# Gathered expert tiles turned by 32x32 block transposes on VectorE instead of on TensorE

## The reference

```python
h = einsum('bsi,boi->bso', x, cond_weight[adapter_ids])          # 1024 x 1024 per batch
shared = silu(h @ Wg_s.T) * (h @ Wu_s.T) @ Wd_s.T                # inner width 1024
probs = softmax(h @ gate_w.T); top 2 of 16, weights normalised
for each expert e:  silu(h @ Wg_e.T) * (h @ Wu_e.T) @ Wd_e.T     # inner width 256
out = x + shared + sum over the token's two experts, weighted
```

## Time and profile before

| | us |
|---|---|
| median of 3 runs (lowest, highest) | 1130.09 (1129.95, 1130.22) |
| span of the profiled execution | 1131.0 |
| TensorE busy | 1108.0 |
| VectorE busy | 567.2 |
| ScalarE busy | 475.7 |
| POOL busy | 166.3 |
| mean traffic of the DMA engines | 219 GB/s |

### The profile page before, as it was taken

The page is one execution under the profiler, slowest core; times in us unless marked ns, Lnnn a source line. Parts: engine busy times, 40 slices in busy tenths (PEclk is TensorE's granted clock), DMA queues, the critical chain, the costliest instruction groups (busy, mean ns, idle before and its releaser), DMA issues.

```text
span 1131.0 us, 16957 instructions
## 1 busy us (share of the span) xinstructions
PE 1108.0 (98%) x5250; PEld 917.4 (81%) x5251; DVE 567.2 (50%) x638; ACT 475.7 (42%) x602; POOL 166.3 (15%) x250
## 2 busy tenths in 40 slices
PE   8999999999999999999999999999999999999996
PEld 7788888888887888888888887788888888888885
DVE  6556555436764445654644544444462355344452
ACT  6556564433233455665645555532331223132210
POOL 1112121000011111111111111041003110032041
PEclk9999999999999999999999999999999999999998
DMA  9787786521256568787786887364256534464264
GB/s 352 291 317 273 266 307 228 198 75 75 89 210 224 191 227 312 252 309 255 293 307 221 310 309 274 124 247 154 92 225 234 213 111 197 156 223 162 79 223 148
DMA packets 40931, 247.45 MB, mean 219 GB/s; under 512 B 4994, under 2 KB 5122, under 8 KB 30594
## 3 DMA queue, kind: packets, MB, share of 16 engines
q1 hardware_dynamic: 14530, 154.15, 36.0%
q0 software_dynamic: 20032, 71.31, 18.4%
q10 hardware_dynamic: 6336, 21.56, 5.1%
HBM read 201.39 MB, written 49.81 MB: 222 GB/s over the span
## 4 chain that ended last, share of the span: by engine, by line
PE 95%; issue 1%; ACT 1%; DVE 1%; DMA 1%; ACTq 0%; DVEq 0%; SPq 0%
PE bank L516 30%; PE bank L518 30%; PE bank L517 29%; PE bank L684 3%; PE bank L537 1%; PE bank L529 1%; PE bank L717 1%; DMA raw<-cond_w 1%; ACT w_split_sb L798 0%; DVE w_split_sb L1050 0%; ACTq L248 0%; ACT y_out L798 0%; ACT hT_hi L798 0%; DVE tile_hT L1050 0%; DVE e_act L1336 0%
## 5 line engine op out<-in xcount | busy, mean ns | idle before, releaser
L1050 DVE TENSOR_TENSOR w_split_sb<-raw,w_split_sb 128x2048 fp32r<-128x2048 f32 (+3 forms) x152 | 259.2, 1728 | 92.9 <-ACT w_split_sb L798 92.0
L798 ACT ACTIVATE w_split_sb<-raw 128x2048 fp32r<-128x2048 f32 (+3 forms) x152 | 218.2, 1463 | 95.3 <-PE bank L518 85.3
L516 PE MATMUL bank<-hT_hi,w_split_sb 128*128 128x512 f32 x512 | 200.0, 391 | 0.9 <-ACT y_out L798 0.9
L517 PE MATMUL bank<-hT_lo,w_split_sb 128*128 128x512 f32 x512 | 199.4, 389 | 0.0
L518 PE MATMUL bank<-hT_hi,w_split_sb 128*128 128x512 f32 x512 | 199.4, 389 | 0.0
L516 PE MATMUL bank<-w_split_sb,tile_hT 128*128 (+1 forms) x312 | 125.7, 403 | 3.8 <-issue 2.6
L518 PE MATMUL bank<-w_split_sb,tile_hT 128*128 (+1 forms) x312 | 122.5, 393 | 0.0
L517 PE MATMUL bank<-w_split_sb,tile_hT 128*128 (+1 forms) x312 | 122.5, 393 | 0.0
L516 PEld LDWEIGHTS bank<-hT_hi,w_split_sb 128*128 128x128 f32 x512 | 96.1, 188 | 21.2 <-issue 1.3
L517 PEld LDWEIGHTS bank<-hT_lo,w_split_sb 128*128 128x128 f32 x512 | 96.1, 188 | 19.9
L518 PEld LDWEIGHTS bank<-hT_hi,w_split_sb 128*128 128x128 f32 x512 | 96.1, 188 | 19.9
(11 more groups left out here) (149 smaller groups left out, 1529.1 us busy)
## 6 DMA issues: line engine op xcount, KB each, us to landing
raw<-sh_gu_w SPq DMA_DIRECT2D x16, 2048.0 KB, 9.0
raw<-exp_gu_w SPq DMA_DIRECT2D x16, 2048.0 KB, 8.7
raw<-cond_w SPq DMA_DIRECT2D x14, 2048.0 KB, 8.6
y_dram<-y_out ACTq DMA_DIRECT2D x39, 512.0 KB, 6.1
raw<-sh_down_w SPq DMA_DIRECT2D x8, 2048.0 KB, 7.9
raw<-exp_down_w SPq DMA_DIRECT2D x16, 1024.0 KB, 7.3
h_dram<-h_row POOLq DMA_DIRECT2D x32, 256.0 KB, 6.0
x_raw_sb<-xT SPq DMA_DIRECT2D x7, 1024.0 KB, 11.0
```

What stands on the lines that cost most here:

```text
L516: nc.tensor.matmul(dst, lhs[0], rhs[0], start=first, stop=False)
L517: nc.tensor.matmul(dst, lhs[0], rhs[1], start=False, stop=False)
L798: return nc.scalar.activation(dst, src, ACT.Copy)
L1050: return nc.vector.tensor_tensor(dst, src, hi.bitcast(F32), ALU.subtract)
```

## The change

The eight transposes per tile leave TensorE. The rows of a tile are gathered in four indirect DMAs: the one with number i brings, to the 32 partitions of group j, quarter j (256 values) of the rows of slots 32 i to 32 i + 31. One VectorE instruction then turns each 32x32 block of the 128x1024 tile, from `h_in[par]` to a new float32 buffer `tile_f32[par]` in the upper half of `raw[1]`. This yields the values of a token along the partitions in another order than before (group j holds quarter j), and the gate-up weights are brought in the same order, by four DMAs of 32 partitions each, every one in runs of 4 KB. ScalarE and VectorE split the turned tile from SBUF in one instruction each, ahead of the silu and the product, and no longer from PSUM. `gather_h` waits for the turn of the tile that last used the buffer. Row numbers (4 x token + quarter) come from four small matmuls with a spreading matrix and one VectorE instruction behind the meta steps (`route_rows`). The last gather, of a tile never used, is left out. The second shared weight load waits for the last tile's split, as the turned tiles share its buffer.

```diff
+            def expert_gu_load(e):
+                by_block = exp_gu_w[bass.ds(e, 1), :, :].rearrange("o (b k) (j n) -> j (o k) b n", k=32, j=BLOCKS)
+                for j in range(BLOCKS):
+                    sp.dma_start(raw[0][32 * j:32 * (j + 1), :].rearrange("k (b n) -> k b n", b=BLOCKS), by_block[j]).then_inc(e_raw_gu, 16)
+
             sp.wait_ge(w_split, POST + 1)
-            sp.dma_start(raw[0][:, :], exp_gu_w[0]).then_inc(e_raw_gu, 16)
+            expert_gu_load(0)
...
             sp.wait_ge(ed_split, EXPERTS)
+            sp.wait_ge(et_lo, 2 * run + 3)
             sp.dma_start(raw[1][:, :], sh_gu_w[1]).then_inc(raw_in[1], 16)
...
-            wait(routed, 1)
+            wait(rows_known, 1)
             wait(a_lo, FB + 2)
             for m in range(2):
                 wait(h_store[m], 16 * QUARTERS * UPQ // 2)
 
+            h_blocks = h_dram.rearrange("t (j c) -> (t j) c", j=BLOCKS)
+
             def gather_h(s, par):
-                wait(et_mm, 2 * s + 2)
-                nc.gpsimd.tensor_copy(idx_h[par][:, :], small["tok_idx"][:, bass.ds(s, 1)]).then_inc(idx_ready, 1)
+                wait(e_turned, s + 1)
+                nc.gpsimd.tensor_copy(idx_h[par][:, :], small["row_idx"][:, bass.ds(s, 1), :].rearrange("p o i -> p (o i)")).then_inc(idx_ready, 1)
                 wait(idx_ready, s + 1)
-                nc.gpsimd.indirect_dma_start(
-                    out=h_in[par][:, :], out_offset=None, in_=h_dram,
-                    in_offset=bass.IndirectOffsetOnAxis(ap=idx_h[par][:, 0:1], axis=0)).then_inc(h_gather[par], 16)
+                for i in range(BLOCKS):
+                    nc.gpsimd.indirect_dma_start(
+                        out=h_in[par][:, i, :], out_offset=None, in_=h_blocks,
+                        in_offset=bass.IndirectOffsetOnAxis(ap=idx_h[par][:, i:i + 1], axis=0)).then_inc(h_gather[par], 16)
 
             gather_h(0, 0)
             gather_h(1, 1)
...
-            def transpose_tile(s, par, count, first_bank=4):
-                pe.wait_ge(h_gather[par], 16 * count)
-                for hf in range(2):
-                    pe.wait_ge(et_lo, 2 * s + hf + 1)
-                    for i in range(4):
-                        k = 4 * hf + i
-                        last = nc.tensor.transpose(bank[first_bank + hf][:, i * P:(i + 1) * P], h_in[par][:, k * P:(k + 1) * P], ident[:, :])
-                    last.then_inc(et_mm, 1)
-
-            def gate_up_tile(s, par, e1, odd, hT_of=None, between=None):
-                pe.wait_ge(et_lo, 2 * s + 4)
+            def spread_tokens(m):
+
+                if m == 1:
+                    pe.wait_ge(rt_tokf, 1)
+                    for i in range(BLOCKS):
+                        last = nc.tensor.matmul(bank[7][:, 128 + i * TPAD:128 + (i + 1) * TPAD], rt["spread"][:, i, :],
+                                                rt["tok_f"][:, :], start=True, stop=True)
+                    last.then_inc(rt_spread, 1)
+
+            def gate_up_tile(s, par, e1, odd, hT_of=None):
+                pe.wait_ge(et_lo, s + 1)
...
-            def tile_step(s, par, nxt_count):
+            def tile_step(s, par):
 
                 (_, e1_before, odd_before), (_, e1, odd) = load_meta(mybir.EngineType.PE, s - 1, 2)
                 gate_up_tile(s, par, e1, odd)
-                transpose_tile(s + 1, 1 - par, nxt_count)
                 down_tile(s - 1, 1 - par, e1_before, odd_before)
                 transpose_act(s, par)
 
-            def first_transposes(m):
-
-                if m == 1:
-                    pe.wait_ge(routed, 1)
-                    transpose_tile(0, 0, 1, first_bank=6)
-
-            shared_down(0, COND_CHUNKS + 4, 0)
-            shared_down(0, COND_CHUNKS + 5, 1, first_transposes)
-
-            def second_transposes():
-                pe.wait_ge(d_ev, 2 * QM + 2)
-                transpose_tile(1, 1, 1)
+            shared_down(0, COND_CHUNKS + 4, 0, spread_tokens)
+            shared_down(0, COND_CHUNKS + 5, 1)
 
             pe.wait_ge(s_mul, FB + 2)
-            pe.wait_ge(routed, 2)
+            pe.wait_ge(routed, 1)
             run = pairs_to_run(pe)
-            gate_up_tile(0, 0, 1, 0, tile0_hT, second_transposes)
+            gate_up_tile(0, 0, 1, 0, tile0_hT)
             transpose_act(0, 0)
             with pe.Fori(0, PAIRS) as i:
                 with pe.If(run > i):
-                    tile_step(2 * i + 1, 1, i + 2)
-                    tile_step(2 * i + 2, 0, i + 2)
-            tile_step(2 * run + 1, 1, run + 2)
-            tile_step(2 * run + 2, 0, run + 2)
+                    tile_step(2 * i + 1, 1)
+                    tile_step(2 * i + 2, 0)
+            tile_step(2 * run + 1, 1)
+            tile_step(2 * run + 2, 0)
 
 
             pe.wait_ge(hT_split, 4)
...
-            def tile_hi(s, dst, first_bank=4):
-                for hf in range(2):
-                    act.wait_ge(et_mm, 2 * s + hf + 5)
-                    copy(dst[:, 0, 4 * hf:4 * hf + 4, :].rearrange("p k t -> p (k t)"), bank[first_bank + hf][:, :]).then_inc(et_hi, 1)
+            def tile_hi(s, par, dst):
+                act.wait_ge(e_turned, s + 3)
+                copy(dst[:, 0, :, :], tile_f32[par][:, :, :]).then_inc(et_hi, 1)
...
+                if not last:
+                    act.wait_ge(gu_mm, s + 2)
+                    tile_hi(s + 1, 1 - par, tile_hT[1 - par])
                 if split_hT:
                     hT_hi_parts(16, (0, 1))
                 silu_tile(s, par)
-                tile_hi(s + 1, tile_hT[1 - par])
                 if split_hT:
...
             def route_tokens():
+                step(nc.vector.tensor_copy(rt["spread"][:, :, :].rearrange("p i (j t) -> p i j t", t=32),
+                                           ident[:, :].rearrange("p (i t) -> p i t", t=32).unsqueeze(2).to_broadcast([P, BLOCKS, BLOCKS, 32])))
                 dve.wait_ge(rt_tok, 1)
-                nc.vector.tensor_copy(small["tok_idx"][:, :], bank[7][:, 64:64 + TPAD]).then_inc(routed, 1)
+                nc.vector.tensor_copy(rt["tok_f"][:, :], bank[7][:, 64:64 + TPAD]).then_inc(rt_tokf, 1)
+
+            def route_rows():
+                dve.wait_ge(rt_spread, 1)
+                nc.vector.tensor_scalar(small["row_idx"][:, :, :].rearrange("p t i -> p i t"),
+                                        bank[7][:, 128:128 + BLOCKS * TPAD].rearrange("p (i t) -> p i t", i=BLOCKS),
+                                        float(BLOCKS), small["block_of"][:, 0:1], ALU.mult, ALU.add).then_inc(rows_known, 1)
 
             def route_start():
                 logits_out(QUARTERS - 1)
...
-            def tile_lo(s, dst, first_bank=4):
-                for hf in range(2):
-                    dve.wait_ge(et_hi, 2 * s + hf + 1)
-                    lo(dst[:, 1, 4 * hf:4 * hf + 4, :].rearrange("p k t -> p (k t)"), bank[first_bank + hf][:, :],
-                       dst[:, 0, 4 * hf:4 * hf + 4, :].rearrange("p k t -> p (k t)")).then_inc(et_lo, 1)
-
-            tile_lo(0, tile0_hT, first_bank=6)
+            def tile_turn(par, count):
+                dve.wait_ge(h_gather[par], 16 * BLOCKS * count)
+                nc.vector.transpose(tile_f32[par][:, :, :].rearrange("p (b a) (i t) -> p i a b t", a=2, t=32),
+                                    h_in[par][:, :, :].rearrange("p i (a b c) -> p i a b c", a=2, c=32)).then_inc(e_turned, 1)
+
+            def tile_lo(s, par, dst):
+                dve.wait_ge(et_hi, s + 1)
+                lo(dst[:, 1, :, :], tile_f32[par][:, :, :], dst[:, 0, :, :]).then_inc(et_lo, 1)
+
+            tile_turn(0, 1)
+            tile_lo(0, 0, tile0_hT)
...
-            def tile_step(s, par, last=False, split_hT=False):
+            def tile_step(s, par, count, last=False, split_hT=False):
                 (new_before, e1_before, odd_before), (new, e1, odd) = load_meta(mybir.EngineType.DVE, s - 1, 2)
                 act_lo(s - 1, 1 - par)
+                if not last:
+                    tile_turn(1 - par, count)
                 with dve.If(new_before == 1):
                     expert_d_lo(2 * WD - odd_before * (2 * WD), 2 * e1_before)
                 if last:
...
                 else:
                     with dve.If(new == 1):
                         expert_gu_lo(2 * CH - odd * (2 * CH), 4 * e1, (0, 1))
+                if not last:
+                    tile_lo(s + 1, 1 - par, tile_hT[1 - par])
                 if split_hT:
                     hT_lo_part(0, 0)
                     hT_lo_part(0, 1)
                 mul_tile(s, par)
-                tile_lo(s + 1, tile_hT[1 - par])
                 if split_hT:
                     hT_lo_part(0, 2)
```

More of the change, by code:

```diff
@@ L94, in adaln_ffn_kernel @@
     tile0_hT = at("tile0_hT", [P, 2, KT, P], F32R, 176)
+    tile_f32 = [at(f"tile_f32{i}", [P, KT, P], F32, 24 + 4 * i) for i in range(2)]
     rows_q3 = [at(f"rows_q3{m}", [P, HID], F32, 144 + 4 * m) for m in range(QM)]
@@ L105, in adaln_ffn_kernel @@
     hT_raw = [at(f"hT_raw{i}", [P, 4, P], F32, 192 + 2 * i) for i in range(4)]
```

(8 more changed lines are left out.)

49 lines of the change are left out of this document (26 added, 23 removed).

## The result

The changed kernel takes 1159.98 us in the median (1152.29 to 1161.69), the kernel before 1130.22 beside it: a ratio of 1.0249, with a 95% interval from 1.0231 to 1.0266. It is slower, and by more than the range allowed. Its profiled execution is the quickest of five, 1152.29 us with a span of 1150.8, so the trace explains 20 of the 30 us; the other four had spans of 1157.9 to 1160.2 us, and no trace of them is there.

The account below looks back on a forecast made before the run. TensorE was taken as the bound (busy 98% of the span, 95% of the chain). Slower gate-up loads, +25.7 us, and removed transposes, -17.4, summed to +8.3 on the median 1130.09: 1138 us, range 1102 to 1150 for 8 in 10.

Parts of the forecast that it names:

- the likeliest case: Gate-up load slowed by about half, making the kernel slower: 1138 us, own range 1126 to 1150, chance 0.55.
- The gate-up load: Four DMAs to 32 partitions take 11 us for 5.5, landing 14.2 us after issue: +25.7 us over eight intervals.
- The eight: Intervals between gate-up load issues behind two-tile experts, 151.1 us together before, forecast at 22.1 us each, 176.8 in all.
- the run length costs nothing: Gate-up load in 4 KB runs for 16 KB: no cost, as y stores in 4 KB runs moved 0.374 MB per us.
- 20 x 0.87 = -17.4 us: Loop steps outside the eight slow cycles and the last two each gain the removed transposes' 0.87 us on TensorE.
- Cost nothing, with 0.2 us of cover: Turn on VectorE in splitting steps: product ready at 8.1 us, TensorE asks for it at 8.3, so no wait.
- ScalarE: "nothing": ScalarE's copy of the turned tile, ahead of the silu, ends at 5.7 us of a step and costs nothing.
- The turn at 1.2 us: VectorE's 128x1024 turn per tile takes 1.2 us, by the nearest row, with bounds of 0.65 and 2.4 us.
- The gathers: "nothing, with 1.9 us of cover": Four gathers per tile on POOL: buffer full after 13.8 us, wanted 15.7 us on, so no cost.
- Rival 3: Late gathers: each of the 20 gaining steps waits 0.6 us for rows, 12 us on top, 1150 us; chance 0.07.
- The clock costs little: TensorE's clock falls when it waits, but the load-and-split loop avoids TensorE, which has 5 us of room per slow cycle.
- rival 1: Gate-up load keeps its full rate, TensorE decides nearly everywhere: -29.6 us, 1100 to 1105 us, 1104 with small waits; chance 0.30.

Follow-up runs that it names:

- mask: Changed kernel with one more register operation per step, bounding the expert number: 1158.68 us, ratio 1.0226.
- parts: Kernel before, each gate-up load cut in four DMAs of 32 partitions in 16 KB runs: 1149.44 us, ratio 1.0171.
- runs: Kernel before, with the changed kernel's gate-up load, four DMAs of 32 partitions in 4 KB runs: 1156.66 us, ratio 1.0225.
- The old order: Changed kernel with silu and product put ahead of the next tile's split again: 1154.14 us; with one 128-partition gate-up load as well, 1125.6 us.
- a quarter of the turn: Changed kernel with one 128-partition load and silu and product ahead of the splits, turning one of four 32-token blocks from the third tile: 1123.57 us, 0.9948.
- best: Changed kernel with one 128-partition load, product before tile splits, its transposes behind register loads, half the down-weight split behind the tile's split: 1116.12 us, 0.9875.
- halves: Second half of the down weights' split moved behind the next tile's split, on the kernel of 1118.71 us: 1116.12 us, 0.9875 against 0.9897 before.
- before, best: Kernel before, with product transposes behind the register loads and the second half of the down weights' split behind the next tile's split: 1127.27 us, 0.9965.

## Why the prediction was wrong

The sign of the likeliest case was right, and the sum was too low: +8.3 us were forecast, and the profiled execution shows +19.8, the medians +29.8.

- **The gate-up load** (+25.7): right in size, in part by luck. The first copy came 14.4 us after the issue for 14.2, a slow interval was 22.1 us for 22.1. The eight sum to +20.3 in the profiled execution and to +26.0 in *mask*'s of usual length. But the 11 us for the transfer were chosen as the middle of two bounds, and "the run length costs nothing" was wrong beside them: *parts* shows 12.7 us to landing for the 32 partitions, *runs* 14.2 with the short runs, and the two errors cancel. (By the prediction's own sum 12.8 us to landing give 1127 us, not 1128.)
- **"20 x 0.87 = -17.4 us"** is the step that failed: outside of the eight intervals the changed kernel is 0.5 us quicker (19.8 - 20.3) in the profiled execution, and 5.1 us slower in *mask*'s. By the starts of their first gate-up matmuls the 20 steps took 189.7 us before and 191.0 after, for a forecast of 172.3; in *mask*'s trace they took 195.8. Of the 18.6 us in which 191.0 misses, nine steps of 9.4 to 10.2 us, with late product and bare register loads, make 12.1; three at a lowered clock (below) 4.2; the first and the last of the 20 make 2.5, and the others come out as forecast. Two premises under it were wrong. (1) *"Cost nothing, with 0.2 us of cover"*: "VectorE starts 2.5 us into the step" was read from one step. The loop makes two steps in an iteration. The row was of an iteration's second step, and in the first one ScalarE starts some 1.3 us later; the trace of before had it too (below). With 3.8 us in place of 2.5 the prediction's own sum gives 9.4 us for the product, 1.1 beyond what TensorE asks for. The text even said that every further tenth would be a wait; the step was right, its input was not. (2) What is behind that wait was not looked at: the next step's register loads on TensorE, hidden so far, come bare behind it. Moving them gave about 6 us.
- **ScalarE: "nothing"**: wrong where it counts. That the copy itself costs nothing may be so, no run has it alone; but with the silu behind it and the low part ahead of the product it made the product late. The old order gives 9.5 us without the slow load, and 4 to 5, not clear of noise, beside it.
- **The turn at 1.2 us**: right (1.24). By *a quarter of the turn*, three quarters of it are worth nothing that can be told in the old order, as the split of the down weights stands ahead of the product all the same.
- **The gathers: "nothing, with 1.9 us of cover"**: wrong, by some 7 to 12 us. The row of 8.1 us to landing was with one gather of 128 packets; in *best*, rows came late by up to 4.3 us. Rival 3 had this mechanism, with a chance of 0.07, but not as it came: of its 20 waits of 0.6 us the changed kernel's trace has three, of 1.8 to 2.6 us, and that its 12 us lie near is chance.
- **"The clock costs little"**: nothing speaks against it in the two-tile intervals, but it was wrong behind them. In the changed kernel six of the steps behind a wait start at a lowered clock, their 24 gate-up matmuls starting over 6.6 to 7.8 us in place of 5.3, and three of these steps are among the 20. One of them, as rows 11:

```profile
527.00:531.00 4.00, 3.65 (x10) 2.89 (x11) 2.47 (x4) 1.97 (x3) 0.00 (x0) 0.57 0.76 225
531.00:537.00 6.00, 6.00 (x28) 4.94 (x27) 3.75 (x4) 2.36 (x4) 3.92 (x5) 1.00 1.03 225
```

  The step from 527.36 to 537.29 took 9.93 us for 8.43. It opens an interval of three tiles, where TensorE has no room: 1.5 us of clock and 1.8 of late product are 3.3 of the 4.0 us by which that interval (29.3) misses its forecast (25.3).

The row that should have been read stood in the trace of the kernel before: ScalarE in two steps in a row, the second of an iteration and the first of the next (TensorE began them at 432.00 and 441.32), and its register loads ahead of them, durations in ns.

```profile
433.89 0.39 ACT L798 ACTIVATE e_aT<-bank 128x256 fp32r<-128x256 f32 x1 [1.23 <-issue]
...
444.67 0.38 ACT L798 ACTIVATE e_aT<-bank 128x256 fp32r<-128x256 f32 x1 [2.52 <-issue]
```

```profile
L248 ACTq TENSOR_LOAD <-meta x1: 547/547/547, 433.3 to 433.3; - x1
```

```profile
L248 ACTq TENSOR_LOAD <-meta x1: 1230/1230/1230, 443.3 to 443.3; - x1
```

ScalarE is idle for 1.23 us ahead of the one, 2.52 ahead of the other; VectorE follows at 445.08, 3.8 us into its step. Of the 1.3 us more, 0.7 are the register load, which takes 1.23 us where it had taken 0.55, and most of the rest is the end of the loop's iteration (its branches, 442.69 to 443.13). At 9.32 us a step this was hidden in both.

What was undone one on top of the other, by the ratios from 1.0226 to 0.9792, each step times 1130 us: load -21.0, order -10.1, register loads -6.1, halves -2.5, gathers -9.4, together -49.1 us. The order and the halves are of this size only on the way taken, and the halves are within the noise. The load was less than half of it. With all of it out of the way (and the rows not where the turn wants them) the time is 1108.4 us, near the 1104 of rival 1, but the register loads and the halves also help the kernel before (*before, best*, 1127.3), so against that the transposes gave back 18.9 us net of their 29.6.

**What stays open.** Why the other four executions took 8 us more than the profiled one; *mask*'s trace, 11.3 us longer, has 5.6 of them in the eight intervals and 4.8 in the 20 steps. How the gathers' cost divides in the changed kernel; in *best* one late gather (5 us) and ScalarE's register loads (2.5) are the largest parts of it. Why the same register load takes 0.55 us in some steps and 1 to 2 us in others: no run took that away.

## What to carry to other kernels

When work is taken off the bounding engine, every slack that was measured against its old step shrinks by that much. Take the cover from the worst of the steps in the trace, not from one that is at hand (here the two kinds alternate, and the worse follows the loop's end), and ask what the engine does right behind a wait that it used to pass: its register loads come bare there. Put ahead of a result that another engine waits for only what is needed as early; and a layout change that confines a DMA to 32 partitions should be bought by laying the data out ahead of time, if it can be.

## What the runs showed of the hardware that was not expected

- Two megabytes in four DMAs of 4 KB runs cost this kernel nothing when each spans 128 partitions (ratio 0.9999, 21442 packets, first queue 37.2%), and 19 us in 16 KB runs when each spans 32 (15298 packets, 41.7%), so that the number of packets does not tell the cost.
- The run length cost time only beside narrow loads: 4 KB instead of 16 KB gave 7 us more over 32 partitions, by 1.5 us more to landing. Over 128 partitions four DMAs of 4 KB runs landed 1.3 us later than one of 16 KB, which this kernel had to spare.
- An indirect DMA occupies POOL as long for rows of 1 KB (0.95 us in the median, up to 1.97) as for rows of 4 KB (0.96 in rows 7), so quarter rows cost some four times as much there: POOL is busy for 312.7 us in place of 166.3.
- TensorE's clock was at half not only at the phase's start: the two windows above show a granted share of 0.57 over 4 us behind 3.48 and 1.29 us of idle time (1.2 in place of 2.4 GHz for most of it), and full speed from 531 on.
- The same register load of ScalarE took 0.55 us in some steps of the kernel before and up to 2.31 in others; four gathers in place of one made it 0.4 us longer (1.97 and 1.55 us in the rows above).
